# Moving the second step of each level of a block inverse behind a piece of probabilities times values, in a two-layer kernel on one core

## What is computed

```python
xn = layernorm(x)
x = x + latent_attention(xn) * silu(mixture_of_experts(xn))   # 16 heads, causal softmax; 8 experts, top 2
xn = layernorm(x)
x = x + ttt(xn) * silu(xn @ sign(weight).T)
```

## Time and profile before

| what | before |
|---|---|
| three runs, us | 597.96, 599.46, 599.63 (median 599.46) |
| the profiled execution's own time | 597.82 |
| its span, first to last instruction | 596.1 |
| PE busy | 564.9 (95%), 7217 matmul records |
| DVE busy | 397.2 (67%) |
| ACT busy | 347.5 (58%) |
| GpSimd busy | 178.4 (30%) |
| mean granted TensorE clock | 0.997 of full |

### The profile page before, as it was taken

How to read it: one execution, slowest core, us unless ns; L and a number is a source line. 1 busy time by engine, 2 the same in 40 slices (tenths; PEclk the granted TensorE clock), 3 DMA queues, 4 the chain that set the end, 5 groups by cost and what they waited for, 6 DMA issues and landing times.

```text
span 596.1 us, 17372 instructions
## 1 busy us (share of the span) xinstructions
PE 564.9 (95%) x7217; PEld 379.4 (64%) x7217; DVE 397.2 (67%) x983; ACT 347.5 (58%) x670; POOL 178.4 (30%) x353
## 2 busy tenths in 40 slices
PE   7789999899999999999999999999999999799797
PEld 3344565467666786677676776668677776555465
DVE  3488766676777876776868676887678676422553
ACT  4421656764758566765667466865676476576231
POOL 7257113222215312341315212532224201411221
PEclk9999999999999999999999999999999999999999
DMA  4766093739153203620253205420262000000001
GB/s 110 167 149 152 10 109 72 137 71 114 34 118 82 64 9 83 137 60 4 55 114 60 63 12 121 96 64 3 64 132 56 21 12 1 27 19 2 2 3 36
DMA packets 58161, 39.41 MB, mean 66 GB/s; under 512 B 17956, under 2 KB 57987, under 8 KB 58083
## 3 DMA queue, kind: packets, MB, share of 16 engines
q1 hardware_dynamic: 58051, 38.29, 31.4%
q10 hardware_dynamic: 32, 0.01, 0.0%
HBM read 24.46 MB, written 9.96 MB: 58 GB/s over the span
## 4 chain that ended last, share of the span: by engine, by line
PE 78%; ACT 9%; DVE 5%; POOL 3%; issue 3%; DMA 1%; SPq 0%; POOLq 0%; DVEq 0%
PE ps_v L963 12%; PE ps_s L944 11%; PE ps_e L925 7%; PE ps_a L879 5%; PE ps_a L865 4%; PE ps_c L1024 4%; PE ps_e L917 3%; PE ps_e L921 3%; PE ps_a L829 3%; PE ps_s L947 2%; PE ps_e L747 2%; ACT hid L1244 2%; ACT prob L1261 2%; PE ps_a L844 2%; PE ps_c L1006 2%
## 5 line engine op out<-in xcount | busy, mean ns | idle before, releaser
L1471 DVE TENSOR_REDUCE cand<-ps_s 128x4 f32<-128x512 f32 (+1 forms) x320 | 212.3, 685 | 49.7 <-PE ps_s L947 30.2
L1261 ACT ACTIVATE prob<-ps_e 128x512 f32<-128x512 f32 x320 | 187.1, 598 | 80.5 <-PE ps_e L925 55.2
L944 PE MATMUL ps_s<-kst,qst 72*128 72x128 bf16 (+2 forms) x1024 | 124.8, 234 | 6.4 <-issue 1.9
L944 PEld LDWEIGHTS ps_s<-kst,qst 72*128 72x128 bf16 (+1 forms) x1024 | 73.9, 98 | 67.5 <-DVE cand L1471 29.7
L925 PE MATMUL ps_e<-qst,kst 75*128 75x256 bf16 (+3 forms) x416 | 104.4, 282 | 0.0
L963 PE MATMUL ps_v<-prob,vaug 128*32 128x512 f32 (+3 forms) x1024 | 87.2, 441 | 0.0
L917 PE MATMUL ps_e<-identb,negmask 128*128 128x150 bf16 (+3 forms) x320 | 72.5, 227 | 4.3 <-ACT prob L1261 4.2
L921 PE MATMUL ps_e<-qst,kst 128*128 128x128 bf16 x384 | 73.9, 219 | 0.0
L925 PEld LDWEIGHTS ps_e<-qst,kst 75*128 75x128 bf16 x416 | 40.5, 97 | 3.6
L747 PE MATMUL ps_e<-identb 128*128 128x512 bf16 x115 | 39.6, 399 | 1.9 <-POOL identb L520 1.9
L947 PE MATMUL ps_s<-negmask,identb 128*128 128x300 bf16 (+1 forms) x128 | 40.6, 317 | 0.0
(11 more groups left out here) (341 smaller groups left out, 901.4 us busy)
## 6 DMA issues: line engine op xcount, KB each, us to landing
qst<-q_scratch SPq DMA_DIRECT2D x48, 192.0 KB
kst<-k_scratch SPq DMA_DIRECT2D x48, 192.0 KB
q_scratch<-qparts SPq DMA_DIRECT2D x24, 128.0 KB, 2.3
k_scratch<-kparts SPq DMA_DIRECT2D x24, 128.0 KB, 2.3
x_res<-in_L_attn_x_dram SPq DMA_DIRECT2D x8, 256.0 KB, 3.1
xn<-in_L_attn_x_dram SPq DMA_DIRECT2D x7, 256.0 KB, 3.6
out_dram<-second SPq DMA_DIRECT2D x7, 256.0 KB, 2.5
max_scratch<-mrow SPq DMA_DIRECT2D x16, 96.0 KB, 2.5
```

The lines of the kernel that those rows point to most:

```text
L944: last = mm(ps_s[:, bank, w * n:w * (n + 1)], q[0:rows, hd, tok(i)], k[0:rows, hd, keys[0]:keys[1]], start=(n == 0), stop=True, skip_group ...
L1261: af(prob[:, u, :], ps_e[:, u % 2, :], ACT.Exp).then_inc(S["e_emptied"], 1)
L1471: vec.tensor_reduce(cand[:, i, h0:h0 + FILLS * (len(hds) - 1) + 1:FILLS, S_SLOT[u]], ps_s[:, u % 2, :].rearrange("p (a c) -> p a c", a=len ...
```

## The change

The table `PLAN` alone is changed; what each piece does, and the tables of the first and the last iteration, are as before.

```diff
-    (1, 4): [...], (1, 5): ["gb3", "lev_a1", "gates"], (1, 6): ["pv0", "gate_norm"], (1, 7): ["lev_d1", "out"], (1, 8): ["c_xn2t"],
-    (1, 9): ["pv1", "lev_a2", "gt"], (2, 0): ["ln1_stats", "lev_d2", "ln1_rstd", "m_parts0"], (2, 1): ["c_ffn"], (2, 2): ["ln1_norm", "lev_a3", "pv2"], (2, 3): ["lev_d3"],
-    (2, 4): ["yt", "m_rows0"], (2, 5): ["lev_a4", "xnt"], (2, 6): ["pv0", "q", "lev_d4"], (2, 7): ["turned0"], (2, 8): ["lev_a5", "k"],
-    (2, 9): ["pv1", "lev_d5", "turned1"], (3, 0): [...], (3, 1): ["lev_a6"], (3, 2): ["h3", "lev_d6", "pv2"], (3, 3): ["c_u0"],
+    (1, 4): [...], (1, 5): ["gb3", "lev_a1", "gates"], (1, 6): ["pv0", "lev_d1", "gate_norm"], (1, 7): ["out"], (1, 8): ["lev_a2", "c_xn2t"],
+    (1, 9): ["pv1", "lev_d2", "gt"], (2, 0): ["ln1_stats", "ln1_rstd", "m_parts0"], (2, 1): ["lev_a3", "c_ffn"], (2, 2): ["ln1_norm", "pv2", "lev_d3"],
+    (2, 4): ["yt", "lev_a4", "m_rows0"], (2, 5): ["xnt"], (2, 6): ["pv0", "lev_d4", "q"], (2, 7): ["turned0"], (2, 8): ["lev_a5", "k"],
+    (2, 9): ["pv1", "lev_d5", "turned1"], (3, 0): [...], (3, 1): ["lev_a6"], (3, 2): ["pv2", "lev_d6", "h3"], (3, 3): ["c_u0"],
```

## The result

| what | before | after |
|---|---|---|
| median of 20 runs, us | 599.38 (596.57 to 605.75) | 603.21 (599.19 to 610.19) |
| ratio, with its 95% interval | | 1.0059 (1.0036 to 1.0083) |
| the profiled execution's span, us | 596.1 | 603.7 |
| tanh of `c_ffn`, first to sixth, us | 151.5 to 478.8 | 157.2 to 486.8 |
| PE busy | 564.9 | 569.3 |

The change makes the kernel slower by 3.5 us (0.6%, interval 2.2 to 5.0 us); forecast was +1.1, within what can be told from no change. The measured 603.2 lies above the range of 597.0 to 602.2. The ratio leaves out runs in a slower state (two of the twenty after), so it comes out a little under the quotient of the medians.

A forecast was written before the change was run, and what follows sets the result against it. PE's own queue was taken to bound the kernel: +0.22 us in each of five full iterations and +0.03 in the sixth, together +1.1 on a mean of 598.7, gave 599.8 us, range 597.0 to 602.2.

The forecast's parts named there:

- Alone among full-array work it costs 0.39 + 0.095 = 0.48: A small-tile step on PE between full-array pieces was to take 0.48 us, beside a `pv` piece 0.39.
- At (3,2) the three changes stay three: At unit (3,2), with `h3`, `lev_d6` and `pv2`, the number of tile-shape changes was to stay the same.
- The four waits: PE waits per full iteration: `lev_d1` 0.12, `lev_a4` 0.06, scores of unit (2,5) 0.32, `k` 0.05; 0.55 us added.
- the wait of `lev_a5` that goes: PE's 0.14 us wait for `lev_d4`'s subtraction on DVE was to vanish, saving 0.70 us over five iterations.
- ACT's copies ... I cost them at nothing: ACT's copies of `lev_a` move by 0.27 us each; idle time on ACT was to cover them, so no cost.
- The wait of unit (2,5): PE's scores of unit (2,5) wait 0.32 us for DVE's reduction of unit (2,3), the largest added term.
- The base: The starting time to which +1.1 us was added: 598.7, the mean of the four executions shown.
- Rival two: DVE's queue from L1566 to unit (2,3)'s reduction is later, 0.4 more a full iteration: +3.1 us, 601.8; chance 0.24.
- Rival one: The added waits stay away as DVE reaches unit (2,3)'s reduction 0.3 earlier: 597.0 on the mean; chance 0.20.
- Rival three: Neighbours of two small shapes pay a further price, so the 1.05 is not saved: +2.2, 600.9 us; chance 0.08.

The follow-up runs named there:

- two of the repairs: Changed kernel with `ln1_norm` moved behind unit (2,3): ratio 1.0032; changed kernel with `lev_a2` behind `c_xn2t` and `lev_a3` behind `c_ffn`: ratio 1.0033.
- the filling in its place: SP's four `load_pads` transfers (unused rows, 256-byte packets) issued where the kernel before has them; seven profiles of the changed order stopped 2.4 to 3.6 us.

## Why the prediction was wrong

1. **"Alone among full-array work it costs 0.39 + 0.095 = 0.48", and "At (3,2) the three changes stay three"**: this step failed. The count of shape changes was right (42 to 40, 0.095 each, 96 ns between `pv` and a step too), but it was not the whole price of adjoining. What stands behind the small tiles mattered as well: a float32 piece loses the early load of its weights, 0.10 us. I had moved three such pieces there (`c_xn2t`, `c_ffn`, `h3`) and took one out of it (`out`). That is +0.21 an iteration, +1.0 us in all, on top of the +1.1 forecast; with the waits of the next point it makes the 2.3 us of the five intervals.
2. **The four waits** came out at 0.60 for 0.55, the largest 0.29 for 0.32, `lev_d1` 0.16 for 0.12. The queue argument on DVE was right, and so was the wait of `lev_a5` that goes.
3. **"ACT's copies ... I cost them at nothing"** held for the time of the copies, but I had overlooked whom `lev_a4` shielded: `xnt`, which shares a bank with `m_rows0`. The wait of unit (2,5) covered that but for 0.03, so the forecast hardly suffered; two of the repairs did.
4. **The base.** 599.8 was put on a mean of 598.7 from four executions; the twenty runs of the kernel before have a median of 599.38. So 0.7 of the 3.4 us between forecast and result is the base.
5. **The rest stays open.** The five intervals explain 2.3 us of the 3.5, which is itself known only to 2.2 to 5.0; 1.2 us are left. The sum was made on one undisturbed execution, and in the first iteration the changed order stopped in each profile with the filling in its place. That could give the rest, but nothing shows that it does: counted in full, stop and clock would give more than 1.2, and other orders that stop as long lie nearer to their periods.
6. Rival two had the right sign and nearly the right time (601.8) for the wrong reason: DVE is hardly later than worked out, and the wait of unit (2,5) is 0.29 for 0.32. Rival one fell: the waits came. Rival three came nearest in kind, since the neighbours of small shapes do pay a further price, though another than the one it named.

Open: why the instruction transfer leaves late with the changed order, and whether the 1.2 us beyond the five intervals are the stop, another cost or noise. No run fixed the place of record 2241 while moving the pieces around it.

## What to carry to other kernels

Moving small-tile matmuls next to each other saves 0.095 us for each change of shape avoided, but look at what then stands behind them: a float32 piece loses its early weight load, 0.10 us, so put bfloat16 work there (0.01), or another small-tile piece. A piece on PE is also cover for a copy between two users of one bank; before moving it, find both. When one wait disappears and the time stays, look at the very next releaser, since it may have been underneath all along.

## What the runs showed of the hardware that was not expected

- PE can run out of instructions. With about 7,000 DMA packets of 256 bytes in flight, one 16 KB instruction transfer left 6 to 8 us late, and PE stopped 1.5 to 3.6 us at the same record, without any wait in the program.
- Such a stop can cost nearly as much again by the clock: at the end of 3.0 us of it the granted clock fell to 1.2 GHz for 6.8 us, and 2.7 us were lost beside the stop. Behind another of 3.2 us it did not fall.
- With the same packets issued later, PE stopped for 8.2 to 10.4 us at the start of the next iteration instead, more than the first stop and its clock had cost.
- Weights of a float32 matmul of the full array were loaded 0.17 us ahead of it behind full-array work, and not ahead at all behind small tiles: 0.10 us a piece.
